# An adaLN Mamba and expert block: the order of work on TensorE and ScalarE rearranged around the gating chain, the batch loop written out

## What is computed

```python
h  = layernorm(x) * (1 + ca) + sa
xi, z = split(h @ in_proj_w.T)                    # 2 x 256 channels
u  = silu(causal_conv4(xi) + conv_b)
dt, Bm, Cm = split(u @ x_proj_w.T, [8, 24])       # rank 8, 16 states
delta = softplus(dt @ dt_w.T + dt_b)
s[t] = s[t-1] * exp(delta[t] * A) + delta[t] * u[t] * Bm[t]   # 256 channels x 16 states
y  = sum_n(s * Cm) + u * D
x  = x + ga * ((y * silu(z)) @ out_proj_w.T)
h  = layernorm(x) * (1 + cb) + sb
w  = top-2 of softmax(h @ router_w + router_b)    # 8 experts
x  = x + gb * (ffn_shared(h) + sum_e w[e] * ffn_e(h))         # hidden 256, exact gelu
```

## Time and profile before

| | us |
|---|---|
| median of 3 runs (lowest, highest) | 762.45 (758.97, 763.31) |
| the profiled run, its own time | 762.81 |
| span of the profiled execution | 761.1 |

### The profile page before, as it was taken

One profiled execution on the slowest core, in us unless ns is written; L12 is line 12 of the kernel. 1 busy time (PEld: TensorE's weight loads), 2 busy tenths in 40 slices (PEclk: granted clock), 3 DMA queues, 4 the chain that ended last, 5 costly groups with the idle time before them and its releaser, 6 DMA issues.

```text
span 761.1 us, 10073 instructions
## 1 busy us (share of the span) xinstructions
PE 615.9 (81%) x3454; PEld 483.1 (63%) x3454; DVE 591.2 (78%) x669; ACT 503.2 (66%) x893; POOL 322.2 (42%) x172
## 2 busy tenths in 40 slices
PE   6737369799869988898869988898979956996697
PEld 4314245579557965678457965778657945695476
DVE  4098998898789997898589997898789898984300
ACT  2475743788578784788378785788578844871363
POOL 1015465445544454345444454345453464553000
PEclk9869559799979989799889989799979977997599
DMA  6413233333421233123422234133432242110000
GB/s 198 175 50 128 110 125 127 112 111 112 139 104 76 112 116 146 65 111 112 140 91 84 114 120 153 57 111 112 142 111 111 112 137 108 71 59 15 0 1 15
DMA packets 26373, 77.84 MB, mean 102 GB/s; under 512 B 2817, under 2 KB 17234, under 8 KB 18130
## 3 DMA queue, kind: packets, MB, share of 16 engines
q1 hardware_dynamic: 25842, 76.75, 27.8%
q10 hardware_dynamic: 480, 0.43, 0.2%
HBM read 74.55 MB, written 2.62 MB: 101 GB/s over the span
## 4 chain that ended last, share of the span: by engine, by line
PE 63%; DVE 15%; ACT 13%; issue 6%; POOL 1%; ACTq 1%; DMA 1%; DVEq 0%; POOLq 0%
PE psum L631 13%; PE psum L483 13%; PE psum L510 8%; DVE state L1082 7%; PE psum L599 4%; PE psum L600 4%; PE psum L601 4%; ACT decay L771 4%; PE psum L641 3%; DVE psum L1073 3%; PE psum L616 2%; PE psum L578 2%; PE psum L528 2%; ACT gT_mix L868 2%; ACT h L902 2%
## 5 line engine op out<-in xcount | busy, mean ns | idle before, releaser
L409 POOL TENSOR_TENSOR state<-state,bc 128x1024 f32<-128x1024 f32 x128 | 302.1, 2360 | 358.7 <-DVE psum L1073 357.4
L1082 DVE TENSOR_TENSOR_SCAN state<-decay,psum 128x1024 f32<-128x1024 f32 x128 | 292.2, 2283 | 17.4 <-PE psum L483 5.5
L483 PE MATMUL psum<-ident,state 128*128 128x128 f32 x1024 | 155.0, 302 | 31.4 <-POOL state L409 31.4
L771 ACT ACTIVATE decay<-delta,a_neg 128x511 f32<-128x511 f32 x256 | 168.6, 726 | 9.2 <-DVE state L1082 9.1
L483 PEld LDWEIGHTS psum<-ident,state 128*128 128x128 f32 x1024 | 135.3, 159 | 49.8 <-POOL state L409 36.7
L1073 DVE TENSOR_TENSOR psum<-bc,du 128x1024 f32<-128x1024 f32 x128 | 157.6, 1231 | 4.7
L631 PE MATMUL psum<-down_w,h 128*128 128x128 f32 x1024 | 125.3, 276 | 0.0
L631 PEld LDWEIGHTS psum<-down_w,h 128*128 128x128 f32 x1024 | 119.2, 192 | 6.1 <-issue 6.1
L902 ACT ACTIVATE h<-psum,vec 128x512 f32<-128x512 f32 x144 | 99.2, 689 | 23.7 <-PE psum L601 22.4
L868 ACT ACTIVATE gT_mix<-psum,w 128x128 f32<-128x128 f32 x256 | 73.3, 373 | 43.0 <-PE psum L641 31.7
L510 PE MATMUL psum<-h_sb,conv_in_wT 128*128 128x512 f32 x128 | 66.4, 670 | 16.6 <-ACT h_sb L781 13.9
(11 more groups left out here) (134 smaller groups left out, 615.0 us busy)
## 6 DMA issues: line engine op xcount, KB each, us to landing
bc<-bc_rows SPq DMA_DIRECT2D x64, 1024.0 KB, 4.7
x_sb<-_attn_hidden_states_dram SPq DMA_DIRECT2D x9, 256.0 KB, 2.9
out_dram<-out_sb SPq DMA_DIRECT2D x8, 256.0 KB, 2.4
x<-_attn_hidden_states_dram SPq DMA_DIRECT2D x7, 256.0 KB, 2.9
h<-in_L_ffn_rw_dram SPq DMA_DIRECT2D x1, 1024.0 KB
bc_rows<-rows SPq DMA_DIRECT2D x8, 64.0 KB, 1.6
h<-in_L_wmod_dram ACTq DMA_DIRECT2D x1, 384.0 KB
h<-in_L_attn_in_proj_w_dram SPq DMA_DIRECT2D x1, 256.0 KB, 4.6
```

Of the source, the lines that this page charges most:

```text
L409: pool.tensor_tensor(state[:, u % STATE_RING, :, :], state[:, u % STATE_RING, :, :], bc[:, pair % BC_RING, 1, first:first + NU, :], ALU.mu ...
L483: last = nc.tensor.matmul(Y[q][:, t * P:(t + 1) * P], state[:, u % STATE_RING, s, t * P:(t + 1) * P], ident[:, :], start=False, stop=(u in ...
L771: last = nc.scalar.activation(decay[:, r, s, 1:L], delta[:, b.p, q, 1:L], ACT.Exp, scale=a_neg[:, q, k:k + 1])
L1082: nc.vector.tensor_tensor_scan(state[:, u % STATE_RING, :, :].rearrange("p n t -> p (n t)"), decay[:, u % DECAY_RING, :, :].rearrange("p n ...
```

## The change

- `pipeline` calls every slot from a Python loop; the hardware loop is gone.
- Set-up: the modulation matmuls stand right behind the conditioning transpose; the transpose of the bias vectors is last on PE, its copy last of the PSUM copies on DVE.
- PE: y_add 15 ahead of x_proj; g_transpose, y_start and out_proj ahead of dt_proj, whose two halves stand around att_transpose; then y_add 0 and both z_proj; y_adds 2, 3 and 4 inside the up block, after k = 2, 8 and 14 (2 stood before it, 3 and 4 after 6 and 14).
- ACT: g_rows and att_rows ahead of softplus relu and abs, which alternate by half; h2_rows ahead of decays 6 and 7; decays 8 behind softplus_log; two decays of n inside the copy loop, h_rows before mix_scaled 6, skip_term behind acc_rows, then decays 3 to 5 of n. z_gate of batch 0 is last in its slot.
- DVE: make_delta after scan 7, and the split of the expert weights ahead of it.

```diff
@@ -258,8 +258,8 @@
-        MM_COND, MM_VEC, MM_MOD, MM_TAPS, MM_PROJ = range(1, 6)
-        EV_MOD, EV_TAPS, EV_PROJ = range(1, 4)
+        MM_COND, MM_MOD, MM_TAPS, MM_PROJ, MM_VEC = range(1, 6)
+        EV_MOD, EV_TAPS, EV_PROJ, EV_VEC = range(1, 5)
...
@@ -280,14 +280,8 @@
             slots(None, None, Batch(0, 0), Batch(1, 1))
-            slots(Batch(0, 0), None, Batch(1, 1), Batch(2, 0))
-            slots(Batch(1, 1), Batch(0, 0), Batch(2, 0), Batch(3, 1))
-            with eng.Fori(2, B - 3, 2) as i:
-                slots(Batch(i, 0), Batch(i - 1, 1), Batch(i + 1, 1), Batch(i + 2, 0))
-                slots(Batch(i + 1, 1), Batch(i, 0), Batch(i + 2, 0), Batch(i + 3, 1))
-            slots(Batch(B - 2, 0), Batch(B - 3, 1), Batch(B - 1, 1), None)
-            slots(Batch(B - 1, 1), Batch(B - 2, 0), None, None)
-            slots(None, Batch(B - 1, 1), None, None)
+            for i in range(B + 1):
+                slots(*(Batch(k, k % 2) if 0 <= k < B else None for k in (i, i - 1, i + 1, i + 2)))
...
@@ -430,18 +424,14 @@
             nc.tensor.transpose(psum[:, 2, 0:B], cond_raw, ident[0:B, 0:B]).then_inc(set_mm, 1)
-            pe.wait_ge(vec_in, 6 * 16)
-            nc.tensor.transpose(psum[:, 3, 0:ROWS], vec_raw,
-                                ident[0:ROWS, 0:ROWS]).then_inc(set_mm, 1)
+            pe.wait_ge(cond_silu, 1)
+            for j, chunk in enumerate((SA, CA, SB, CB, GA, GB)):
+                last = nc.tensor.matmul(MOD[:, j * B:(j + 1) * B],
+                                        wmod_sb[:, chunk * DM:(chunk + 1) * DM], condT,
+                                        start=True, stop=True)
+            last.then_inc(set_mm, 1)
             def setup():
-                pe.wait_ge(cond_silu, 1)
-                for j, chunk in enumerate((SA, CA, SB, CB, GA, GB)):
-                    last = nc.tensor.matmul(MOD[:, j * B:(j + 1) * B],
-                                            wmod_sb[:, chunk * DM:(chunk + 1) * DM], condT,
-                                            start=True, stop=True)
-                last.then_inc(set_mm, 1)
...
@@ -460,6 +450,10 @@
                 last.then_inc(set_mm, 1)
+                pe.wait_ge(vec_in, 6 * 16)
+                nc.tensor.transpose(psum[:, 3, 0:ROWS], vec_raw,
+                                    ident[0:ROWS, 0:ROWS]).then_inc(set_mm, 1)
...
@@ -529,12 +523,11 @@
-            def dt_proj(n):
+            def dt_proj(n, q):
                 pe.wait_ge(bcdt_done, n.i + 1)
-                for q in range(Q):
-                    nc.tensor.matmul(A[q], dt_wT[2 * NS:2 * NS + R, q, :],
-                                     bcdt[2 * NS:2 * NS + R, :], start=True,
-                                     stop=True).then_inc(dt_done, 1)
+                nc.tensor.matmul(A[q], dt_wT[2 * NS:2 * NS + R, q, :],
+                                 bcdt[2 * NS:2 * NS + R, :], start=True,
+                                 stop=True).then_inc(dt_done, 1)
...
@@ -660,37 +653,36 @@
                     y_add(a, UN - 2)
+                    y_add(a, UN - 1)
                 if n:
...
                 if a:
-                    y_add(a, UN - 1)
-                if n:
-                    dt_proj(n)
-                if a:
                     g_transpose(a, n)
...
                     y_start(b)
+                if a:
+                    out_proj(a)
+                if n:
+                    dt_proj(n, 0)
+                if a:
+                    att_transpose(a)
+                if n:
+                    dt_proj(n, 1)
+                if b:
                     y_add(b, 0)
-                if a:
-                    out_proj(a)
                 if n:
                     z_proj(n, 0)
-                if a:
-                    att_transpose(a)
-                if n:
                     z_proj(n, 1)
...
                     router(a)
-                if b:
-                    y_add(b, 2)
                 for k in range(M_UP):
...
                         up(a, n, k)
-                    if b and k in (6, 14):
-                        y_add(b, 3 + k // 14)
+                    if b and k in (2, 8, 14):
+                        y_add(b, 2 + (k - 2) // 6)
                 if a:
...
@@ -786,6 +778,8 @@
                     act.wait_ge(input_done, (n.i - 1) * UN)
+                if q == 0 and n.i == 0:
+                    act.wait_ge(set_ev, EV_VEC)
                 act.wait_ge(conv_done, Q * n.i + q + 1)
...
@@ -815,21 +809,17 @@
-            def softplus_relu(n):
-                for q in range(Q):
-                    act.wait_ge(dt_done, Q * n.i + q + 1)
-                    nc.scalar.activation(delta[:, n.p, q, :], A[q], ACT.Relu,
-                                         bias=vec[:, ROW_DTB + q:ROW_DTB + q + 1]
-                                         ).then_inc(sp_relu, 1)
-            def softplus_abs(n, b):
+            def softplus_relu(n, q):
+                act.wait_ge(dt_done, Q * n.i + q + 1)
+                nc.scalar.activation(delta[:, n.p, q, :], A[q], ACT.Relu,
+                                     bias=vec[:, ROW_DTB + q:ROW_DTB + q + 1]).then_inc(sp_relu, 1)
+            def softplus_abs(n, q, b):
                 if b:
                     act.wait_ge(skip_acc, b.i + 1)
-                for q in range(Q):
-                    act.wait_ge(dt_done, Q * n.i + q + 1)
-                    nc.scalar.activation(skip[:, q, :], A[q], ACT.Abs,
-                                         bias=vec[:, ROW_DTB + q:ROW_DTB + q + 1]
-                                         ).then_inc(sp_abs, 1)
+                act.wait_ge(dt_done, Q * n.i + q + 1)
+                nc.scalar.activation(skip[:, q, :], A[q], ACT.Abs,
+                                     bias=vec[:, ROW_DTB + q:ROW_DTB + q + 1]).then_inc(sp_abs, 1)
...
@@ -908,25 +898,23 @@
                     bcdt_rows(n)
-                    softplus_relu(n)
                 if a:
                     g_rows(a, n)
-                if n:
-                    softplus_abs(n, b)
-                if a:
                     att_rows(a)
-                if n:
+                for q in range(Q):
+                    if n:
+                        softplus_relu(n, q)
+                        softplus_abs(n, q, b)
+                if n and n.i > 0:
                     z_gate(n)
+                if n:
                     softplus_exp(n, a)
...
                     load_exp_table(a)
+                    h2_rows(a)
                 if b:
...
                     decays(b, AHEAD + 1)
-                if a:
-                    h2_rows(a)
-                if b:
-                    decays(b, AHEAD + 2)
                 if a:
...
@@ -935,33 +923,28 @@
                     softplus_log(n)
-                for j in range(6):
+                if b:
+                    decays(b, AHEAD + 2)
+                for j in range(DOWNS - 1):
                     if b:
                         decays(b, AHEAD + 3 + j)
+                    if n and j in (4, 5):
+                        decays(n, j - 4)
+                    if m and j == 6:
+                        h_rows(m)
                     if a:
                         mix_scaled(a, j)
-                if b:
-                    decays(b, UN - 1)
+                if n:
+                    decays(n, 2)
+                if a:
+                    mix_scaled(a, DOWNS - 1)
+                    acc_rows(a)
                 if n:
                     skip_term(n)
-                    decays(n, 0)
-                if a:
-                    mix_scaled(a, 6)
-                if n:
-                    decays(n, 1)
-                if m:
-                    h_rows(m)
-                if n:
-                    decays(n, 2)
-                if a:
-                    mix_scaled(a, 7)
-                if n:
-                    decays(n, 3)
-                if a:
-                    acc_rows(a)
-                if n:
-                    for u in range(4, AHEAD):
+                    for u in range(3, AHEAD):
                         decays(n, u)
+                    if n.i == 0:
+                        z_gate(n)
...
@@ -973,8 +956,6 @@
             def setup():
-                dve.wait_ge(set_mm, MM_VEC)
-                nc.vector.tensor_copy(vec[:, :], psum[:, 3, 0:ROWS])
                 dve.wait_ge(taps_in, 2 * 16)
...
@@ -1013,6 +994,8 @@
                 last.then_inc(set_ev, 1)
+                dve.wait_ge(set_mm, MM_VEC)
+                nc.vector.tensor_copy(vec[:, :], psum[:, 3, 0:ROWS]).then_inc(set_ev, 1)
...
@@ -1229,9 +1212,13 @@
                     xhat(m)
+                if n and n.i == 0:
+                    split_up_weights()
                 if b:
...
                     scan(b, 7)
+                if n:
+                    make_delta(n)
                 for u in range(8, UN):
...
@@ -1240,10 +1227,6 @@
                         scan(b, u)
-                    if n and u == 8:
-                        make_delta(n)
```

(50 more changed lines are left out.)

## The result

The changed kernel takes 770.62 us (median of 4 runs, 768.74 to 772.36) against 762.88 (4 runs): ratio 1.011, interval 1.0069 to 1.0151. It is slower by 1.1%, 6.6 us above the forecast of 764 and inside its range of 752 to 774. The profiled execution spans 770.6 us; that run took 772.36.

A forecast was written before the change was run, and what follows sets the result against it. No engine is full; PE is the thread, waiting for x1hat and mix_scaled. Slot 1 at 106.6, five slots totalling 426, slot 6 +4.8 and slot 7 -0.5 gave span 763.0, forecast 764 us, range 752 to 774.

The forecast's parts named there:

- The chain behind the last mix_add: End of a slot: late skip_term holds delta_x, input 13, readout 12, y_add 12; next conv_in 9.6 us after mix_add 7.
- The full slot: Slots 1 to 5, one pipeline pass each: 85.2 us forecast, against 83.8 before without the loop's edge.
- The rival without a tail chain: End of a slot: late skip_term does not hold PE; slot 78 us, total some 725; chance 0.05.
- The front: Gating chain, x1_transpose and router up to the up block: earlier by 2.0 to 2.3 us a slot.
- The clock: Up block: PE's short pauses still drop the clock, costing about 2.0 us there against 2.5 before.
- the rival of a clock that stays up: Up block: the shorter pauses no longer drop the clock; 12 us less, 752; chance 0.2.
- The cold start of conv_in: Rival at slot start: after 7 us idle PE the clock returns only at C+4 to C+6; +9, 773; chance 0.2.
- The loop's edge: Back edge of the hardware loop: writing it out removes a 2.73 us stall plus 0.4 of slower conv_in.
- Set-up and slot 0: Work before slot 1: 6.2 us saved in sum, so conv_in of slot 1 starts at 106.6 instead of 112.8.
- it now begins near 41.5: Slot 0: conv_in of batch 1 starts there instead of 49.62, removing DVE's 2.91 us wait before scan 4.
- Slots 6 to 8: Last slots: slot 6 takes 4.8 us more, slot 7 0.5 less, slot 8 unchanged.
- the forecast case: Whole kernel: the summed forecast of 764 us holds, own range 757 to 770; chance 0.55.

The follow-up runs named there:

- e1: Changed kernel with skip_term moved from behind acc_rows to right behind decays 15, ahead of h_rows and mix_scaled 6: 730.25 us.
- e3: Changed kernel with delta_x after scan 14 instead of scan 12, waits of scans 14 and 15 raised, skip_term left late: 729.47 us.
- e4: Kernel before the change with only skip_term moved behind acc_rows: 798.70 us.
- e7: Changed kernel with PE's pauses filled by 6 identity transposes ahead of x1_transpose and 20 between it and router, results unused: 759.15 us.
- e5: Kernel before the change with only the hardware loop written out: 759.78 us.
- e2: Changed kernel with z_gate of batch 0 behind softplus_log instead of last in its slot: 766.77 us.
- e10: Changed kernel with z_gate of batch 0 behind softplus_log, skip_term in the copy loop ahead of decays 12, waits of scans 14 and 15 raised: 723.48 us.
- e8: Changed kernel with the edits of e2 and e3 together: 722.92 us.
- e9: Changed kernel with the edits of e8 plus the filler transposes of e7: 722.88 us.

## Why the prediction was right or wrong

**The chain behind the last mix_add: right in place and price.** It was put at 9.6 us from mix_add 7 to conv_in, through acc_rows, skip_term, delta_x, input 13, readout 12 and y_add 12, with 6 us of waiting on DVE and 7 on PE. Measured: 9.6, 5.97 and 6.97. Taken away from either end (e1, e3) it gives 40 us back; put alone into the kernel before (e4) it costs 36. The full slot was forecast at 85.2 and measured at 85.1. The rival without a tail chain, 725, is out: that is about what the kernel takes when the chain is freed (e1, e3), not as it stands.

**The front: right, near enough.** Counted from the chain's start of the slot, 453.57, as the prediction counted: x1_transpose was forecast at C+24.3 and came at C+24.6, the router at C+27.0 and C+27.6, mix_add 7 ended at C+76.0, not C+75.6. So all of it is 0.3 to 0.6 us late, of which 0.4 is conv_in: it took 4.79 us in this slot and 4.36 before. The two pauses were forecast at 1.3 and 2.2 and are 0.68 and 2.27; the wait of g_transpose for bcdt_rows, 0.8, is 0.77. DVE's wait for softplus_log, forecast at 0.8, is 0.73 to 0.86 in slots 1 to 5 and 3.23 in slot 6.

**The clock: right.** It fell in the up block, and e7 prices that at 11.5 us in all; the rival of a clock that stays up had 12 us for it. The cold start of conv_in was priced as a rival at 9 us more; at the start of slot 6 it was cold from C-2.6 to C+2.4 (536.5 to 541.5), against C+1.6 in the sum and C+4 to C+6 in the rival. Conv_in's extra over the 3.60 us of full clock is 1.1 to 1.5 us in slots 3 to 6, where C+1.6 makes an estimated 0.8. This rival did not come true, and its 773 lies nearer to the measured 770.6 than the forecast does: that is chance.

**The loop's edge: right.** 3.1 forecast, 3.5 measured (e5).

**Set-up and slot 0: wrong, and this is the miss.** The step that failed is "it now begins near 41.5". Of the waits of conv_in of batch 1 only h_rows was taken into account. The same few lines hold a wait for zs_done of the batch before, for n = 1 and 2, and the change moves z_gate of batch 0 to the end of ACT's slot. So conv_in began at 51.23, DVE's wait before scan 4 grew from 2.91 to 6.05 instead of going, and slot 1 started at 113.64, not 106.6: 7.0 us late, against 7.6 between the forecast span of 763.0 and the measured 770.6. Of the 7.0, the wait that was to go is 6.05, and delta_x of batch 0 is 1.05: it came at 45.15, 2.3 earlier than before and not 3.35. Of the 1.2 us of set-up 0.2 is seen at conv_in of batch 0 (14.90, was 15.11). e2 shows the cause of the wait: with z_gate back, conv_in of batch 1 starts at 40.05, the wait is gone, and 3.9 us come back by the medians, 5.6 by the profiled spans. In the tail the prediction followed a moved step to all who wait for its semaphore; here it followed z_gate only along its own chain.

**Slots 6 to 8: nearly right.** +4.8 was forecast for slot 6 and 4.5 measured; behind it 0.5 less was forecast and 0.7 more came, which was not followed up.

Because the miss was in a single event and the term that recurs was right, the sum stayed within 1%. It did leave the forecast case's own range of 757 to 770 by 0.6 us; that the stated range still holds it is owed to the room given to the cold start, which did not happen. The sign was left open, with chances of 0.31, 0.35 and 0.34. In these a slip stands: the last rival, at 725, would be all faster, but 0.02 of its 0.05 is counted as same. By the sum's arithmetic the kernel would have been level with the one before without the miss; e2, which takes the miss out, is still 0.6% slower (1.0033 to 1.0082).

## What to carry to other kernels

When a step is moved, list every wait on its semaphore, and for each waiting engine what stands in line behind that wait; in this kernel a late producer cost nothing by itself (e3), and 40 us in front of the wrong queue entry. Where one semaphore counts work of two batches, an order that looks arbitrary may be what keeps a consumer from starting on the wrong count. And price a filler or a clock only against what bounds the version at hand: the same 26 transposes a slot were worth 11.5 us and then nothing that could be measured.

## What the runs showed of the hardware that was not expected

26 transposes of the identity a slot, put into idle time and thrown away, made the changed kernel 1.5% faster: the granted clock stays at 1.00 into the up block where it was 0.57 on average over the 7.8 us from behind x1_transpose. Once the tail was freed, a mean clock of 0.70, 0.83 or 1.00 over the 10 us from the router's start (e10, e8, e9) made no difference in time. After the pause of about 7 us before y_add 12, the first half of conv_in took between 3.73 us (e4, at 293.29) and 5.13 us (e7, at 445.73), against 3.60 at full clock: the same pause is followed by a cold start of different length. Writing out a hardware loop of two iterations with two slots each took 3.5 us off, of which 2.73 was one stall of PE.
